# A GRU and expert-choice kernel on one core: expert matmuls of 256 columns in every second time step instead of 128 columns in every step

## What is computed

```python
def cell(h, x):                      # 256 times, one after the other
    gi = x @ W_ih + b_ih             # (16,512) @ (512,1536)
    gh = h @ W_hh + b_hh
    i_r, i_z, i_n = jnp.split(gi, 3, axis=-1)
    h_r, h_z, h_n = jnp.split(gh, 3, axis=-1)
    r = sigmoid(i_r + h_r); z = sigmoid(i_z + h_z)
    n = jnp.tanh(i_n + r * h_n)
    return (1.0 - z) * n + z * h
...
S = softmax(xf @ router_w + router_b)            # xf: 4096 tokens x 512
G, idx = jax.lax.top_k(S.T, k)                   # 16 experts, k = 256
out = jnp.einsum('ekh,hd->ekd', xf[idx], expert_w) + expert_b
y = zeros.at[idx].add(G[..., None] * out)
return x + y
```

## Time and profile before

| | |
|---|---|
| three runs | 1194.54 us median, 1192.84 to 1197.85 |
| profiled execution | 1198.08 us, its span 1196.3 us |
| PE | busy 1159.9 us (97%), 28983 matmul records |
| PE weight loads | busy 965.6 us (81%) |
| VectorE | busy 767.9 us (64%) |
| ScalarE | busy 360.9 us (30%) |
| time steps 0 to 255 | from about 19 to 1109 us of the span |
| search and combination | from about 1109 to 1193 us |
| DMA queue of kind "instruction" (q8) | 226 packets, 3.70 MB |

### The profile page before, as it was taken

One profiled execution on the slowest core, in us unless ns is written; L12 is line 12 of the kernel. 1 busy time (PEld: TensorE's weight loads), 2 busy tenths in 40 slices (PEclk: granted clock), 3 DMA queues, 4 the chain that ended last, 5 costly groups with the idle time before them and its releaser, 6 DMA issues.

```text
span 1196.3 us, 64639 instructions
## 1 busy us (share of the span) xinstructions
PE 1159.9 (97%) x28983; PEld 965.6 (81%) x28983; DVE 767.9 (64%) x4248; ACT 360.9 (30%) x1367; POOL 6.4 (1%) x28
## 2 busy tenths in 40 slices
PE   5999999999999999999999999999999999899887
PEld 2778888888888888888888888888888888788776
DVE  1666666666666666666666666666666666566886
ACT  1233232333333232333323232333323232232430
POOL 2000000000000000000000000000000000000000
PEclk9999999999999999999999999999999999999999
DMA  8200000000000000000000000000000006400008
GB/s 245 64 7 9 12 13 12 12 13 12 12 7 9 12 12 13 12 12 12 13 7 9 13 13 12 12 13 12 12 10 5 12 12 157 121 4 4 21 29 257
DMA packets 86356, 37.40 MB, mean 31 GB/s; under 512 B 75712, under 2 KB 75712, under 8 KB 86080
## 3 DMA queue, kind: packets, MB, share of 16 engines
q1 hardware_dynamic: 80576, 28.69, 10.4%
q10 hardware_dynamic: 5504, 4.59, 1.4%
HBM read 24.87 MB, written 8.39 MB: 28 GB/s over the span
## 4 chain that ended last, share of the span: by engine, by line
PE 91%; DVE 5%; issue 1%; DMA 1%; SPq 1%; ACT 0%; DVEq 0%
PE gates L403 56%; PE gates L388 26%; PE ffn_ps L442 6%; DVE wih L665 2%; PE gates L442 2%; DMA whh<-in_L_cond_W_hh 1%; PE log_ps L451 1%; DVE u L564 0%; ACT th L306 0%; DVE zT L571 0%; SPq L214 0%; DVE tok L589 0%; DVE z_h L576 0%; DVE nT L580 0%; DVE reached L681 0%
## 5 line engine op out<-in xcount | busy, mean ns | idle before, releaser
L403 PE MATMUL gates<-whh,tok 128*16 128x192 f32 x16384 | 727.6, 329 | 9.8 <-DMA whh<-in_L_cond_W_hh 4.9
L403 PEld LDWEIGHTS gates<-whh,tok 128*16 128x16 f32 x16384 | 563.4, 125 | 111.7 <-DVE tok L589 7.7
L388 PE MATMUL gates<-wih,xT 128*32 128x192 f32 x8192 | 386.2, 329 | 9.1 <-DMA wih<-in_L_cond_W_ih 8.2
L564 DVE SCALAR_TENSOR_TENSOR u<-th,gates 128x64 f32<-128x64 f32 x512 | 112.6, 220 | 341.1 <-ACT th L306 341.1
L388 PEld LDWEIGHTS gates<-wih,xT 128*32 128x32 f32 x8192 | 268.3, 111 | 76.9 <-DVE xT L536 7.7
L306 ACT ACTIVATE th<-gates 128x128 f32<-128x128 f32 x512 | 137.4, 268 | 486.6 <-PE gates L403 486.6
L311 ACT ACTIVATE n_t<-v 128x64 f32<-128x64 f32 x512 | 131.5, 257 | 277.8 <-DVE v L568 277.8
L442 PE MATMUL ffn_ps<-we,tok 128*32 128x128 f32 x2816 | 128.9, 281 | 3.7 <-issue 3.7
L580 DVE STREAM_TRANSPOSE nT<-n_t 128x64 f32<-128x64 f32 x512 | 123.9, 242 | 0.0
L571 DVE STREAM_TRANSPOSE zT<-th 128x64 f32<-128x64 f32 x512 | 122.0, 238 | 0.0
L568 DVE SCALAR_TENSOR_TENSOR v<-u,gates 128x64 f32<-128x64 f32 x512 | 113.2, 221 | 8.8
(11 more groups left out here) (103 smaller groups left out, 135.6 us busy)
## 6 DMA issues: line engine op xcount, KB each, us to landing
x_in<-in_x SPq DMA_DIRECT2D x256, 32.0 KB, 2.3
xs<-in_x SPq DMA_DIRECT2D x30, 256.0 KB, 7.9
out<-tok SPq DMA_DIRECT2D x16, 256.0 KB, 4.9
out<-tok ACTq DMA_DIRECT2D x16, 256.0 KB, 4.8
whh<-in_L_cond_W_hh SPq DMA_DIRECT2D x4, 768.0 KB, 9.8
wih<-in_L_cond_W_ih SPq DMA_DIRECT2D x4, 512.0 KB, 7.5
wih<-in_L_cond_W_ih SPq DMA_DIRECT2D x4, 256.0 KB, 6.7
we<-in_L_ffn_expert_w SPq DMA_DIRECT2D x1, 1024.0 KB, 5.5
```

Source lines behind the costliest of these rows:

```text
L388: nc.tensor.matmul(gates[q % 2][a][Q * j:Q * (j + 1), IN:HN].rearrange("b (g k c) -> b g k c", g=G, k=KH), xT[:, n % 2, kc, first:first + ...
L403: mm = nc.tensor.matmul(gates[t // S % 2][a][Q * j:Q * j + rows, R_:GC].rearrange("b (g k c) -> b g k c", g=G, k=KH), columns, by_tile(whh ...
L564: V.scalar_tensor_tensor(u[a][:, :], th[a][:, 0, :], 1.0, ps[a][:, HN:GC], ALU.add, ALU.mult).then_inc(u_ready[a], 1)
```

## The change

A unit now has 256 moving columns (a half of the outputs in place of a quarter), UNITS is 8, and the call in the time loop stands in even steps only. FIRST stays 16, IN_LOOP stays 15, and the numbers of units in the search are halved, so that each place after the loop gets the same number of columns as before.

```diff
-    UNITS = K * 4
-    FIRST = T - IN_LOOP * UNITS
+    UNITS = K * 2
+    SPAN = 2 * UNITS
+    FIRST = T - IN_LOOP * SPAN
     BANKS = 5
 
-    SOFTMAX_UNITS, ROUND_UNITS, SHORT_UNITS = 32, 8, 4
+    SOFTMAX_UNITS, ROUND_UNITS, SHORT_UNITS = 16, 4, 2
...
-                if t > FIRST and (t - FIRST) % UNITS == 0:
-                    store_ffn((t - FIRST) // UNITS - 1)
-                if t >= FIRST and (t - FIRST) % UNITS == 2 and (t - FIRST) // UNITS + 1 < IN_LOOP:
-                    preset_ffn((t - FIRST) // UNITS + 1)
+                if t > FIRST and (t - FIRST) % SPAN == 0:
+                    store_ffn((t - FIRST) // SPAN - 1)
+                if t >= FIRST and (t - FIRST) % SPAN == 2 and (t - FIRST) // SPAN + 1 < IN_LOOP:
+                    preset_ffn((t - FIRST) // SPAN + 1)
...
-                    n, kc, quarter = unit // UNITS, unit % UNITS // 4, unit % 4
+                    n, kc, half = unit // UNITS, unit % UNITS // 2, unit % 2
                     unit += 1
-                    cols = slice(quarter * P, (quarter + 1) * P)
-                    if kc == 0 and quarter == 0:
+                    cols = slice(half * D // 2, (half + 1) * D // 2)
+                    if kc == 0 and half == 0:
                         pe.wait_ge(ffn_preset, n + 1)
...
-                    if kc == K - 1 and quarter == 3:
+                    if kc == K - 1 and half == 1:
                         mm.then_inc(ffn_done, 1)
...
-                if t >= FIRST:
+                if t >= FIRST and s == 0:
                     expert(1)
```

## The result

The changed kernel took 1209.2 us (median of 4 runs, 1208.2 to 1211.5) beside 1195.9 us for the kernel before (4 runs, 1192.8 to 1197.9): a ratio of the means of 1.0116, with a 95% interval from 1.0087 to 1.0146. It is slower, as forecast, but by 13.3 us and not by the 22.2 us of the sum, and 1209.2 lies just under the low end of the range, 1210. The prediction was wrong.

What follows compares the result with a forecast made beforehand. The prediction took the time loop to wait for its state, with PE's work ending together with it. The loop's +24.2 us less 2.0 us at the end gave +22.2, so 1216.7 us against a median of 1194.54; range 1210 to 1223.

Steps and rivals of the forecast that it cites:

- What bounds the loop: Time loop: each step waits for the state, 4.16 us even and 4.19 us odd, though PE reads 97% busy.
- the hole: PE's 0.23 us in each time step between projection and next recurrence, which the narrow unit fills to within 0.01 us.
- the second rival: Time loop: the odd step makes good the even one's overrun, so the loop stays; 1192.5 us, chance 2%.
- The price of a wide unit: Expert unit of 256 columns: 0.433 us for its 8 records, with ends 0.428 and 0.442 us.
- The first rival: Expert units: weight loads, not columns, set the pace; wide unit 0.22 us, total 1191 us; 5% together with 1197.3 us case.
- The even step: Time loop, step with the wide unit: 0.203 us longer, 4.36 us, set by PE alone.
- The odd step: Time loop, step without a unit: stays at 4.19 us, its hole empty and the overrun not made good.
- The end: Last stretch and units after the loop: fewer instruction fetches and 0.6 us of units gain 2.0 us, ends 0 and 3.5.
- The cap from the stores: Last stretch: stores at 336 GB/s keep the end from coming before about 1193 us in place of 1196.3.
- The stops in the loop: PE's issue stops where x is loaded again: their places are chance, 0 plus or minus 3 us.
- The clock: Time loop: empty holes of 0.2 us in odd steps don't lower the granted clock of 1.00; zero.
- The third rival: Fetches gain more: 3.5 us at the end, 3 us where x is loaded; +17.1 us, 1211.6 us, chance 12%.

Runs made afterwards that it cites:

- the last run: Kernel before with wide units after the time loop only and the second loads of x spread tile by tile over the loop: 1188.3 us, ratio 0.9933.

## Why the prediction was wrong

**What bounds the loop: right.** The steps wait for the state, the hole is 0.23 us, and PE's 97% hides that. The narrow unit costs nothing, and the second rival (only PE's total counts) is out: the loop got longer with the same columns, and the run with two narrow units shows the same with the same matmuls.

**The price of a wide unit: right.** 0.43 us was forecast and 0.43 to 0.44 measured. The run with 512 columns gives 0.86 us for eight records, so from 128 to 512 columns the time goes with the columns (0.22, 0.27, 0.33, 0.43 and 0.86 us at 128, 160, 192, 256 and 512). The first rival is out, and with it the Trainium skill's figures in "TensorE: Matmul & The Clock Gate", section "Back-to-back issue gap": the measured ratio for four times the columns is 0.86 to 0.22, 3.9, and not 131 to 81, 1.6. The trace disagrees for these float32 matmuls of 32 stationary columns.

**The even step: right**, 4.36 us forecast and measured.

**The odd step: this is the term that was mis-sized.** The prediction said "So 4.19 us as before, and the overrun isn't made good". The odd step takes 4.13 to 4.14. I counted the 4.19 us from a recurrence that waits for its state and took them for one that doesn't. There the first weights are loaded before the matmuls' turn and the block is 0.05 us shorter. The term 119 x 0.203 = 24.2 us measured 119 x 0.144 = 17.1, which is 7.1 of the 10.1 us by which the two profiled spans (12.1 us apart, where the medians are 13.3) differ less than the sum. Its range (23.6 to 25.2) took in only the price of the unit, and nothing for the length of a step that starts late.

The row for it was in the trace of before. The router block pushes seven even steps past their hole, and the prediction wrote of the odd one after it that it "keeps 4.19". It never had 4.19. Around t = 32 and 33 PE's timeline of the kernel before reads:

```profile
165.25 0.40 PE L442 MATMUL ffn_ps<-we,tok 128*32 128x128 f32 x8
165.47 2.78 PE L403 MATMUL gates<-whh,tok 128*32 128x192 f32 x64
168.06 1.48 PE L388 MATMUL gates<-wih,xT 128*32 128x192 f32 x32
...
169.60 2.81 PE L403 MATMUL gates<-whh,tok 128*16 128x192 f32 x64
```

The odd step takes 4.13 us (165.47 to 169.60), and all seven lie between 4.13 and 4.14. Only these seven pairs grow by the full price, 0.21 us (9.15 to 9.37 us); the ordinary ones grow by 0.14. With this row the sum would have been 17.1 - 2.0 = +15.1 us, or 1209.6 against the same median.

**The end: right in size, and the reason holds for the stops.** 2.0 us were taken and 2.6 came in the profiles. The stops of 1.14 and 2.52 us went, as in both runs with wide units after the loop, and they came back in all six runs with narrow ones (single stops of 0.17 to 2.51 us). How much this is worth varies. The wide ends are 34.0, 34.3 and 34.1 us long, the narrow ones 36.6, 36.4, 35.8, 34.9, 35.8, 33.3 and 35.2. The shortest of them, that of the run with 192 columns, is under the wide ones; its granted clock is 1.00 in the first 5 us of the end, where the nine other profiles have 0.66 to 0.69. The cap from the stores wasn't tested by itself, but the changed kernel's end fits it: its DMA engines stay full after the last scaling.

**The stops in the loop: within the bounds, by luck.** They were put at 0, plus or minus 3, and gave 1.5 us back. The run with wide units in the loop only has the same loop and stops of 5.3 us there, 1.2 more than before, so the sign was chance. That they come from the burst of loads is shown by the last run: with the burst spread, they are gone. That PE waits there for instructions is borne out by the packets of the instruction queue, whose late landings the stops follow; no run moved the fetches alone.

**The clock: right in the loop.** Empty holes of 0.2 us left it at 1.00 from 100 to 1000 us. The 1.1 us of the search weren't foreseen and aren't from the change.

The sum with the measured terms is 17.1 - 2.6 - 1.1 - 1.5 = 11.9 us; the leftovers are +0.35 and -0.2, and the spans differ by 12.1. The third rival's number, 1211.6 us, came nearest of all, but not by its mechanism: it kept 23.6 us for the loop and reached its time by larger gains at the end and at the loads.

## What to carry to other kernels

In a loop that waits for its own result, work costs nothing only up to the hole of the step in which it stands; put twice as much into every second step and the excess is paid, less the 0.03 to 0.05 us that the next block saves by not waiting, while the other hole stays empty. Measure the hole by starts of like instructions with and without the filling, not by busy shares. When a step is pushed past its hole, price it with a block that didn't have to wait, since that block is a little shorter, and so the true limit lies a little beyond the hole that the waiting steps show. Look for such a block in the trace that you have: any step that is already overlong, like the router steps here, is followed by one.

## What the runs showed that was not expected

- A block of 64 records of 192 columns takes 2.60 us to the next block when its stationary operand is there in time, with 16 and with 32 columns alike. When PE has to wait for it, it takes 2.62 to 2.63 us with 16 columns and 2.65 to 2.66 us with 32.
- Because of that, units of 160 columns in every step are nearly as cheap as units of 128 (+2.2 us for 25% more columns, ratio 1.0017 with 1 inside the interval), though they are 0.04 us longer than the hole.
- Thirty loads of 256 KB in a row cost PE 2.6 to 6.0 us in stops that name no cause but issue, and in some of the profiles a few us at half clock besides. The stops follow 16 KB packets of the instruction queue that land late, 8 us apart in place of 5. The same loads spread over the loop cause no stop.
